# A gate's small matmuls replaced by row products on VectorE and sums on VectorE and ScalarE

## The reference

```python
A = M / (jnp.sum(M, axis=0, keepdims=True) + EPS)     # two graph layers over adj, 4096 x 4096
W = jnp.where(A > THRESH, A, 0.0)
agg = einsum('ji,jd->id', W, h @ W_in + b_in) / (sum(W, axis=0)[:, None] + EPS)
out = agg @ W_out + b_out + (h @ W_self + b_self);  h = relu(layernorm(out) * gamma + beta)
...
x = x + gnn(layernorm(x), adj)
logits = layernorm(x) @ gate_w + gate_b                # 8 experts
idx = argmax(softmax(logits)); pos = running count of the rows that chose idx, this one included, less one
buf[idx, pos] = x   (dropped from place 640 on);  y = expert(buf) taken back, times the probability
...                                                    # then adj @ (layernorm(x) * W), then a routed block of 16 experts
```

## Time and profile before

| | |
|---|---|
| median of 3 runs | 989.96 us (989.27 to 991.37) |
| the profiled execution | 987.18 us, its span 985.4 us |
| PE busy | 959.8 us, 97% |
| DVE busy | 519.1 us, 53% |
| ACT busy | 318.9 us, 32% |
| POOL busy | 188.8 us, 19% |
| first layer | to about 297 us, 36.35 us a block |
| second layer | to 538 us, 29.45 us for each of blocks 1 to 7 |

### The profile page before, as it was taken

How to read it: one execution, slowest core, us unless ns; L and a number is a source line. 1 busy time by engine, 2 the same in 40 slices (tenths; PEclk the granted TensorE clock), 3 DMA queues, 4 the chain that set the end, 5 groups by cost and what they waited for, 6 DMA issues and landing times.

```text
span 985.4 us, 15370 instructions
## 1 busy us (share of the span) xinstructions
PE 959.8 (97%) x4814; PEld 553.0 (56%) x4822; DVE 519.1 (53%) x1519; ACT 318.9 (32%) x628; POOL 188.8 (19%) x216
## 2 busy tenths in 40 slices
PE   8999999999999999999999799989999999999997
PEld 4455554554554544444444388834566666666665
DVE  6424324323423243444443388557867867867854
ACT  3654554555541010000000154414143242242332
POOL 3110010010010122112222236443101201202101
PEclk9999999999999999999999899989999999999999
DMA  9996675376204688888778357637998999989841
GB/s 356 422 424 221 274 332 229 137 318 255 87 1 171 249 342 297 333 297 324 295 294 335 108 157 247 216 92 269 408 342 321 352 319 336 356 333 330 292 143 52
DMA packets 64479, 262.73 MB, mean 267 GB/s; under 512 B 8836, under 2 KB 24904, under 8 KB 52102
## 3 DMA queue, kind: packets, MB, share of 16 engines
q1 hardware_dynamic: 61254, 257.16, 69.3%
q0 software_dynamic: 2864, 4.39, 1.3%
q10 hardware_dynamic: 272, 0.13, 0.0%
HBM read 243.85 MB, written 20.01 MB: 268 GB/s over the span
## 4 chain that ended last, share of the span: by engine, by line
PE 83%; DVE 7%; issue 3%; ACT 2%; DVEq 2%; DMA 1%; POOL 1%; ACTq 0%; another core or an unknown queue 0%; SPq 0%; POOLq 0%
PE PA L1789 21%; PE PA L1809 20%; PE PA L2046 16%; PE O L1984 3%; PE O L2150 3%; PE O L1858 3%; ACT U L778 2%; PE O L1830 2%; PE T L2159 1%; PE SM L2150 1%; PE SR L2150 1%; PE PA L1776 1%; PE O L1820 1%; PE O L2127 1%; PE SR L2172 1%
## 5 line engine op out<-in xcount | busy, mean ns | idle before, releaser
L1809 PE MATMUL PA<-ring,S 128*128 128x512 f32 x512 | 227.3, 592 | 2.1 <-DMA ring<-in_adj_cols 1.6
L1789 PE MATMUL PA<-ring,U 128*128 128x512 f32 x512 | 226.1, 595 | 0.1
L1789 PEld LDWEIGHTS PA<-ring,U 128*128 128x128 f32 x512 | 94.9, 190 | 107.2 <-issue 107.1
L1809 PEld LDWEIGHTS PA<-ring,S 128*128 128x128 f32 x512 | 95.7, 190 | 103.7 <-issue 99.0
L2047 PE MATMUL PA<-ring 128*64 128x256 f32 x560 | 130.8, 380 | 0.0
L698 ACT ACTIVATE work<-ring 128x2048 int8<-128x2048 f32 x64 | 122.2, 1910 | 8.9 <-issue 4.7
L2046 PE MATMUL PA<-ring,S 128*64 128x256 f32 x448 | 105.2, 380 | 0.5 <-DVE ring L1634 0.5
L2046 PE MATMUL PA<-ring 128*64 128x256 f32 x336 | 81.2, 381 | 0.0
L2046 PEld LDWEIGHTS PA<-ring,S 128*64 128x64 f32 x448 | 60.5, 137 | 35.6 <-issue 6.5
L2047 PEld LDWEIGHTS PA<-ring 128*64 128x64 f32 x560 | 75.5, 137 | 0.0
L2046 PEld LDWEIGHTS PA<-ring 128*64 128x64 f32 x336 | 44.9, 137 | 24.2 <-issue 2.4
(11 more groups left out here) (298 smaller groups left out, 1345.1 us busy)
## 6 DMA issues: line engine op xcount, KB each, us to landing
ring<-in_adj_cols SPq DMA_DIRECT2D x52, 2048.0 KB, 9.4
ring<-in_adjT_cols SPq DMA_DIRECT2D x32, 2048.0 KB, 9.6
ring<-w_d SPq DMA_DIRECT2D x128, 256.0 KB, 4.0
ring<-in_adj_cols SPq DMA_DIRECT2D x8, 1024.0 KB, 12.4
ring<-in_Wr SPq DMA_DIRECT2D x4, 2048.0 KB, 10.2
w_d<-ring SPq DMA_DIRECT2D x8, 1024.0 KB
work<-in_w SPq DMA_DIRECT2D x16, 256.0 KB
disp_d<-U SPq DMA_DIRECT2D x4, 650.0 KB, 19.5
```

Source lines behind the costliest of these rows:

```text
L1789: mm = nc.tensor.matmul(out_T[:, :], X[:, t * D:(t + 1) * D], ring[slot][t // HT][:, (t % HT) * BW:(t % HT + 1) * BW], start=n == 0, stop= ...
L1809: mm = nc.tensor.matmul(PA[k % 2][:, :], S[:, t * D:(t + 1) * D], ring[slot][t // HT][:, (t % HT) * BW:(t % HT + 1) * BW], start=t == 0, s ...
```

## The change

- For the blocks k = 1 to 7 (`BY_ROWS`) the logits are no longer made by PE. `gate_products(k, x1, t)` runs on DVE for each of the four tiles: two multiplications of 128x512 (the tile's row repeated four times, by four rows of the gate's weights each), and a sum of the second product over 128 columns (128x512 to 128x4). The first product is summed by ACT, in four ACTIVATE instructions of 128x128 with an accumulator output. The four calls stand around the moments and the normed rows in `route`; tiles 2 and 3 wait for ACT's sums of tiles 0 and 1, whose buffers they take.
- `tail_b`, ACT's copy `hnT` and `tail_c` stay for k = 8 alone; `tail_d` moves from product 25 to product 28.
- `mask2(k + 1)` moves from ahead of `route(k)` to behind the choice, ahead of the wait for the counts (`s_cum`).
- The gate's weights are loaded once more as `gate_rows`, 8 x 128 numbers in each of the 128 partitions (512 KB), in `tail_inputs`.
- `load_weights(0, 0)` waits for the last use of the buffers by block 7's choice (`s_l2`), and stands between the second and the third load of `Wr`.
- In `L1_PIECES`, `empty_cols`, `out_rows` and `turn_z` stand one product later (5, 9, 19), and `self_rows` of the first step too (6); `layer2_products` stays at 22.

```diff
+        gate_rows = part(at, E1 * D)
+        gate_part = [part(at, BW), hnT, msk]
+        BY_ROWS = range(1, NB)
@@ SP: tail_inputs, and the loads after the last block
+                sp.dma_start(gate_rows, A["gate_rows"]).then_inc(s_gate_rows, 16)
-            load_weights(0, 0)
             for n, q in enumerate(ORDER2):
+                if n == 2:
+                    sp.wait_ge(s_l2, NB - 1)
+                    alone(sp)
+                    load_weights(0, 0)
@@ ACT: step2
+                if k in BY_ROWS:
+                    for t in range(BT):
+                        act.wait_ge(s_gate_part, (k - 1) * BT + t + 1)
+                        alone(act)
+                        for i in range(E1 // 2):
+                            some = gate_part[t % 2][:, i * D:(i + 1) * D]
+                            at = t * E1 + i
+                            last = nc.scalar.activation(some, some, ACT.Copy, accum_out=lg[:, at:at + 1])
+                        last.then_inc(s_gate_sum, 1)
+                else:
+                    act.wait_ge(s_hn2p, 1)
+                    nc.scalar.copy(hnT, T[1][:, :]).then_inc(s_hn2T, 1)
@@ DVE
+            def gate_products(k, x1, t):
+                half = E1 // 2
+                x1_t = x1[t].unsqueeze(1).to_broadcast([P, half, D])
+                if k == 1 and t == 0:
+                    dve.wait_ge(s_gate_rows, 16)
+                    alone(dve)
+                if t >= 2:
+                    dve.wait_ge(s_gate_sum, (k - 1) * BT + t - 1)
+                    alone(dve)
+                nc.vector.tensor_tensor(tiles(gate_part[t % 2], half), x1_t, tiles(gate_rows[:, 0:half * D], half), ALU.mult).then_inc(s_gate_part, 1)
+                nc.vector.tensor_tensor(tiles(gate_part[2], half), x1_t, tiles(gate_rows[:, half * D:E1 * D], half), ALU.mult)
+                dve.drain()
+                nc.vector.tensor_reduce(lg[:, t * E1 + half:(t + 1) * E1], tiles(gate_part[2], half), AX.X, ALU.add)
+                dve.drain()
@@ DVE: route(k)
+                if k in BY_ROWS:
+                    gate_products(k, x1, 0)
                 lnorm_stats(lambda t: x1[t])
+                if k in BY_ROWS:
+                    gate_products(k, x1, 1)
...
+                    gate_products(k, x1, 2)
                     normed_rows(x1, range(BT))
+                    gate_products(k, x1, 3)
...
+                    dve.wait_ge(s_gate_sum, k * BT)
+                    nc.vector.tensor_tensor(e3(lg), e3(lg), bce(rstd[:, 0:BT]), ALU.mult)
...
                 nc.vector.reciprocal(rows3[:, :, D], esum)
                 dve.drain()
+                if k < NB - 1:
+                    dve.wait_ge(s_thr2[k % 2], (k + 1) // 2 * 16)
+                    alone(dve)
+                    mask2(k + 1, k % 2, (k + 1) // 2 * 16 + 64)
                 dve.wait_ge(s_cum, k)
@@ DVE: step2
                 add_branch(k)
-                dve.wait_ge(s_thr2[slot], n_rnd * 16)
-                alone(dve)
-                mask2(k + 1, slot, n_rnd * 16 + 64)
                 route(k)
@@ PE
-            L1_PIECES = ((2, turn_h, 0), (4, empty_cols, 1), (8, out_rows, 1), (18, turn_z, 1),
+            L1_PIECES = ((2, turn_h, 0), (5, empty_cols, 1), (9, out_rows, 1), (19, turn_z, 1),
                          (22, layer2_products, 1), (28, self_rows, 0))
-                step(k, L1_PIECES if k > 1 else L1_PIECES[:2] + ((5, self_rows, 1),) + L1_PIECES[2:])
+                step(k, L1_PIECES if k > 1 else L1_PIECES[:2] + ((6, self_rows, 1),) + L1_PIECES[2:])
@@ PE: step2
                 tail_a(k)
-                products(U, sl, 2, 16, s_quart2, ROWS2, slot)
-                tail_b(k)
-                products(U, sl, 16, 19, s_quart2, ROWS2, slot)
-                tail_c(k)
-                products(U, sl, 19, 25, s_quart2, ROWS2, slot)
+                products(U, sl, 2, 28, s_quart2, ROWS2, slot)
                 tail_d(k)
-                products(U, sl, 25, NT, s_quart2, ROWS2, slot).then_inc(s_agg2, 1)
+                products(U, sl, 28, NT, s_quart2, ROWS2, slot).then_inc(s_agg2, 1)
```

More of the change, by code:

```diff
@@ L166, in build @@
         rb4 = part(at, 4)
-        assert at + 4 <= WORK
+        at += 4
+        gate_rows = part(at, E1 * D)
+        at += E1 * D
+        gate_part = [part(at, BW), hnT, msk]
+        assert at + BW <= WORK
+        BY_ROWS = range(1, NB)
         at = 0
@@ L380, in build @@
         s_lg = sem("s_lg")
+        s_gate_rows = sem("s_gate_rows")
+        s_gate_part = sem("s_gate_part")
+        s_gate_sum = sem("s_gate_sum")
         s_gsum = sem("s_gsum")
@@ L746, in step2 @@
                 nc.scalar.copy(p2T, PA[1 - slot][:, :]).then_inc(s_p2, 1)
-                act.wait_ge(s_hn2p, k)
-                nc.scalar.copy(hnT, T[1][:, :]).then_inc(s_hn2T, 1)
+                if k in BY_ROWS:
[10 more added lines that the diff above has]
+                    nc.scalar.copy(hnT, T[1][:, :]).then_inc(s_hn2T, 1)
                 if k == NB:
@@ L1334, in route @@
                 else:
+                    gate_products(k, x1, 2)
                     normed_rows(x1, range(BT))
+                    gate_products(k, x1, 3)
                 dve.drain()
                 nc.vector.tensor_tensor(shift, gbc, shift, ALU.subtract)
-                dve.wait_ge(s_lg, k)
-                alone(dve)
-                nc.vector.tensor_tensor(e3(lg), e3(SR[:, 0:BT * E1]), bce(rstd[:, 0:BT]), ALU.mult)
+                if k in BY_ROWS:
+                    dve.wait_ge(s_gate_sum, k * BT)
+                    alone(dve)
+                    nc.vector.tensor_tensor(e3(lg), e3(lg), bce(rstd[:, 0:BT]), ALU.mult)
+                else:
+                    dve.wait_ge(s_lg, 1)
+                    alone(dve)
+                    nc.vector.tensor_tensor(e3(lg), e3(SR[:, 0:BT * E1]), bce(rstd[:, 0:BT]), ALU.mult)
                 if k < NB:
@@ L1897, in tail_c @@
             def tail_c(k):
-                pe.wait_ge(s_hn2T, k)
+                pe.wait_ge(s_hn2T, 1)
                 for t in range(BT):
@@ L2283 @@
         "gate_w": g["L0_ffn_gate_w"],
+        "gate_rows": bc(_np.ascontiguousarray(g["L0_ffn_gate_w"].T)),
         "g2_bc": bc(g["L0_gnn_g2"]),
```

## The result

The changed kernel took 979.17 us (median of 4 runs, 978.07 to 981.06), the kernel before 989.62 us in the same comparison: 0.9894 of it, with a 95% interval of 0.9877 to 0.9912. Forecast were 979.1 us.

A forecast was written before the change was run, and what follows sets the result against it. PE was taken as the bound, busy 97% of the span. Gains of 8.75 us (second layer) and 2.2 us (first layer) make 10.9: 987.2 - 10.9 = 976.3 us, stated as 979.1 since timed runs lie 2.8 us higher; range 977.5 to 986.0.

The forecast's parts named there:

- PE's rows, 1.25 us a block: Second layer, blocks 1 to 7: tail_b (0.44 us) and tail_c (0.81 us) leave PE; 8.75 us in all.
- The gate call, 2.15 us: Each gate_products call on DVE: two multiplications and a sum, 0.61 + 0.77 + 0.77 us; 8.60 us for four.
- Slower: Rival: DVE's repeated-row multiplication or 3-dimensional sum runs at half rate, 0.53 us more each; about 1007 us; chance 0.05.
- ACT's sums, 0.43 us each and a tie: Second layer: four ACT sums take 1.7 us; ACT done at 19.65, DVE's own work at 19.66; 0.2 us of waiting.
- The choice at 21.9 us: Second layer: DVE's choice comes 21.9 us after tail_a, PE wants it at 22.35; margin 0.45 us, no wait.
- The mask, L1369 at 24.6, the places at 25.8, POOL free at 31.55: Second layer, behind the choice: mask gap 1.91 us, then DVE's places, then POOL's four scatters, at these times after tail_a.
- The loop: Second layer: DVE and POOL, from power through four scatters to the next power, 28.0 us beside PE's 28.2.
- Block 8's end at no cost: End of second layer, k = 8: POOL free at 30.2, half a us before its power is due; priced at nothing.
- The first layer, 2.2 us: First layer: empty_cols one product later ends its waiting for DVE's L1073; gain 7 x 0.22 + 0.65 = 2.2 us.
- The second loop as a rival: Rival, second layer: DVE and POOL's chain is 0.5 to 1.2 us longer and takes over; 981 to 985 us; chance 0.22.
- POOL and DVE block each other: Rival, in route: DVE must let POOL's power end first, chain 0.7 to 1.04 us longer; 982.6 to 985 us; chance 0.13.

The follow-up runs named there:

- r1_after: The changed kernel, unchanged, run again in the third set: 974.57 us, ratio 0.9897 to the kernel before.
- e3_late_wait: Changed kernel with DVE's wait for the landed scatter moved behind the first two gate products and the moments: 977.38 us, ratio 0.9875 to the kernel before.
- e6: Changed kernel with the last sum of 128x512 made twice, 0.77 us more on DVE's chain: 977.95 us, ratio 0.9925 to the kernel before.
- e7: e3_late_wait's kernel with the last sum of 128x512 made twice, 0.77 us more on DVE's chain: 971.84 us, ratio 0.9855 to the kernel before.
- e5_tail_d_25: Changed kernel with tail_d put back after product 25: 986.8 us, ratio 1.002 to the kernel before.

## Why the prediction came out right, step by step

- *PE's rows, 1.25 us a block.* Measured 1.33. The durations were right; the 0.08 us of gap that stood beyond 12 products behind `tail_c` went as well. 7 x 1.33 = 9.3, of which block 4 gave back 0.3: 9.01.
- *The gate call, 2.15 us.* Measured 2.12. The sum over 512 numbers, which had no row, took 0.69 us as a multiplication does, and so did the multiplications with a repeated row; nothing ran at half the rate, which answers the rival *Slower*. In groups of DVE and ACT by line and form:

```profile
L1352 DVE TENSOR_REDUCE work<-work 128x4 f32<-128x512 f32 x28 | 19.2, 686 | 2.4 <-issue 0.4
```

```profile
L766 ACT ACTIVATE work<-work 128x128 f32<-128x128 f32 x112 | 33.2, 297 | 106.7 <-DVE work L1349 106.7
L766 ACT ACTIVATION_READ_ACCUMULATOR work<-work 128x1 f32 x112 | 20.9, 187 | 0.0
```

- *ACT's sums, 0.43 us each and a tie.* A term that was mis-sized. The timeline of ACT shows that the reading of one sum runs under the next one, so a sum costs 0.29 us:

```profile
407.57 0.29 ACT L766 ACTIVATE work<-work 128x128 f32<-128x128 f32 x1
407.77 0.19 ACT L766 ACTIVATION_READ_ACCUMULATOR work<-work 128x1 f32 x1
407.86 0.29 ACT L766 ACTIVATE work<-work 128x128 f32<-128x128 f32 x1
408.06 0.19 ACT L766 ACTIVATION_READ_ACCUMULATOR work<-work 128x1 f32 x1
```

  ACT is done with the last tile at 408.54, and DVE's L1386, which needs the sums, starts at 408.77 in its turn. No wait of DVE for ACT's sums shows in this execution (one of 0.2 us in `r1_after`).
- *The choice at 21.9 us.* Measured 21.77 in block 3 and right for the wrong reason. Of it 0.56 us is waiting for the scatter and 0.24 for POOL's power; without the landing's wait it is there at 409.84 - 388.91 = 20.93 (`e3_late_wait`). The chain's own work was over-estimated by 1.0 us: 0.3 ahead of `route` (mostly a wait for POOL of 0.56 us in block 3 of the old trace, which is 0.33 elsewhere), 0.25 by the wait for ACT that isn't there, the rest by fulfilled waits priced too high.
- *The mask, L1369 at 24.6, the places at 25.8, POOL free at 31.55.* Measured in block 3 24.59, 25.78 and 31.56, right by the same compensation as the choice, from which they are counted. The gap of the mask was 2.04 us, against 1.91; in blocks 1 and 4 to 6 it was 1.67 to 1.68.
- *The loop.* This is the step that failed. The prediction closed the loop through POOL's queue and the power. The same four scatters close it a second time, through their landing and DVE's wait for `s_sc` at the head of `route`, which the section on the kernel names and the sum never priced. From POOL's last instruction to DVE's going on it took 396.96 - 392.82 = 4.1 us in block 3 and 5.2 us in block 4, and the wait now sat right behind L1336, some 2 us earlier than where the mask had kept it. It cost 0.3 us in one block and 1.3 to 2.0 us between the last `tail_a` and the last `tail_d` (14.10 and 14.85 us against 12.82 without it), where I had written that nothing was due. `e3`, `e6` and `e7` show it. The table's line for this stretch has only 0.69 us, since 0.8 us came back behind `tail_d` in this execution.
- *Block 8's end at no cost.* The sentence on POOL was right (its power waited 0.96 us for DVE, where half a us was stated, and not the other way); the landing was left out of it.
- *The first layer, 2.2 us.* Measured 2.85. I took 0.08 us of each delay for a change of the operand's kind. The changed kernel has none there: `empty_cols` follows its products exactly. The whole 0.30 was waiting, 8 x 0.30 and 0.44 for the missing transposes make 2.84.
- *The second loop as a rival.* Its price was added up wrongly: blocks of 28.5 to 29.2 us beside 28.2 cost 2.1 to 7.0 us, not 1.7 to 5.7, which makes 981.2 to 986.1 us. In the changed kernel this loop did not set the pace.
- *POOL and DVE block each other.* Not so for DVE: its multiplications beside the power start 0.60 us apart like the others. POOL's power of `route` takes 1.28 us in blocks 1 to 7 and 1.01 in block 8, where DVE is idle beside it; so POOL is held by 0.27 us, all of it covered by the second gate call:

```profile
400.84 1.28 POOL L970 TENSOR_TENSOR small<-small,neg_half 128x4 f32<-128x4 f32 x1 [6.79 <-DVE small L1291]
...
539.18 1.01 POOL L970 TENSOR_TENSOR small<-small,neg_half 128x4 f32<-128x4 f32 x1 [5.30 <-DVE small L1291]
```

  The Trainium skill (SBUF — State Buffer, Who interferes with whom) says that a VectorE instruction with two SBUF inputs contends with a GpSimd instruction that reads SBUF, for ports that one of the two holds exclusively. The direction agrees with the trace, the size does not: a full block by the multiplication ahead would hold POOL for most of its 0.69 us and a block of DVE for 1.0; the measured 0.27 decides.
- *What could not be seen beforehand.* The start's 2.2 us in this one execution. By the medians the change is worth 10.45 us in the comparison that gave the result, 9.3 us in the first set and 11.3 us in the third.

What is left open: the 0.5 us between the profiles in the third and fourth part, where nothing was changed and other pairs of kernels differ by as much; what the medians show of the landing beyond the traces; and whether more warming products ahead of the first quarter would keep the start at its shorter length, which wasn't tried.

## What to carry to other kernels

When work moves to an engine that has room, follow every loop that this engine is part of, and close each through all of its returns: an indirect DMA comes back as the queue that issued it and as the landing that frees its buffer, and the second is the longer and the less steady. A wait that frees a buffer belongs directly ahead of the first write to that buffer; here moving it by two calls was worth 2.8 to 2.9 us by the medians (1.2 to 2.6 us of it seen in the traces) and made the chain insensitive to 0.77 us more work. A wait of PE can cost more than its length: price what the granted clock does behind it too. Where a stage's timeline shows a wait of a few tenths that repeats exactly in each block, all of it is waiting until a row shows otherwise.

## What the runs showed of the hardware

- An indirect DMA of 128 rows, issued by POOL while the ring's loads kept the DMA engines 78 to 97% busy, took 3.5 to 6.6 us from the end of POOL's instruction to DVE's going on (27 waits of DVE in seven profiles; the longest in `e5_tail_d_25`, 5.2 us in block 4 of the changed kernel). At the end of block 8 of the kernel before, with the loads done, SP went on 560.69 - 559.49 = 1.2 us after POOL's last one. What makes the difference was not separated.
- Five waits, a register load and a branch that isn't taken cost DVE 1.7 to 2.1 us where the profile names nothing that it waited for (the gap ahead of L1422).
- Beside DVE's instructions with two SBUF inputs, POOL's power over 128x4 takes 1.28 us in place of 1.01, while DVE keeps its pace.
- PE's granted clock from 9 to 20 us is 1.00 in the profiles where PE had idled up to 1.7 us in front of the first product, and 0.84 to 0.86 where it had idled 2.0 us or more; the start is then some 2 us longer. In the middle of the kernel it was 0.82 for the 9.5 us behind a wait of 2.2 us (`e5_tail_d_25`, block 2), which made 18 matmuls 1.7 us longer, and 1.00 behind waits of 0.7 to 1.1 us.
